# TensorE's order of an edge-gated graph layer, spread over one more block of edges

## The chip, the cores and the metric

One core of a Trainium2 chip runs the whole program. The metric is the device time of one execution in microseconds, the median of the runs. The engines are named as in the profile: PE (TensorE, matmuls), PEld (its weight loads), DVE (VectorE), ACT (ScalarE), POOL (GpSimd), SP (SyncE, which issues DMAs).

## The reference

A graph of 12,500 nodes (64 features) and 412,500 edges (32 features), sorted by destination. Cut to what matters:

```python
h  = relu(layernorm(x))
h0 = edge_attr @ W0 + b0
t  = gelu(gelu(h0) @ W1 + b1) @ W2 + b2
score = (h0 + t) @ W3 + b3                 # one row of 64 per edge
msg   = h[src] * score
sums  = segment_sum(msg, dst); cnt = segment_sum(1, dst)
out   = x + (sums / max(cnt, 1)) @ Wo + bo
```

## The kernel before

The edges are cut into NB = 403 blocks of 1,024 (8 tiles of 128). W2 and W3 are folded into one matrix `w_last` at the start. The layer norm of all nodes is made first and stored to `h_dram`; then the blocks are worked through one after the other. For block b:

- `first(b)` (PE, line 438): W0 times the block's attributes, into one of two PSUM banks `ps_h0a`, `ps_h0b` by parity. It raises `h0_done`. ACT's first gelu (line 392) turns it into `g1`.
- `second(b)` (PE, line 444): W1 times `g1`, into `ps_h1a`, `ps_h1b`. It raises `h1_done`. ACT's second gelu (line 397, two halves) writes rows 0 to 63 of `act_in`; the attributes themselves lie below them.
- `last(b)` (PE, line 453): 8 pairs of weight load and matmul that make the scores in `ps_sa`, `ps_sb`. It raises `score_done`. DVE multiplies them with the gathered rows of h (`message`, line 638) and raises `msg_done`.
- `summed(b)`, here `narrow` (PE, lines 465 and 472): waits for `msg_done` of b and for `added` of b - 1, then sums the messages of the block over a window of 64 destinations with a one-hot matrix (DVE, line 630), two tiles per matmul, into the one PSUM bank `ps_w`, and counts with two more matmuls. It raises `sums_done`. DVE's `add_window` (lines 739 to 750) adds the bank to the accumulator `acc` in SBUF and raises `added`.
- POOL gathers the 1,024 rows of h of a block with 8 indirect DMAs (line 334), into a ring of 16 blocks. The 8 gathers of block b + 16 wait for `msg_done` of b and for `score_done` of b + 8: so POOL may be at most 8 blocks ahead of the scores.
- SP loads the attributes twice, as `pair` (for `first`) and as rows of `act_in` (for `last`), each into a ring of 4.

The order on each engine is written out by hand and all waits are on semaphores. PE runs its steps in a loop of four blocks per turn. In a step b, PE does `second(b)`, `first(b + 1)`, `summed(b - 1)`, `last(b)`. DVE does one-hot of b, `add_window(b - 1)`, `message(b)`. ACT does the first gelu of b, then the second of b. After block 391 (EARLY_BLOCKS) PE projects the finished nodes (`project_early`), and then the last 12 blocks are worked through; the last gathers lie just after that projection.

## Time and profile before

| | |
|---|---|
| median of 3 runs | 4828.14 us (4825.08 to 4829.34) |
| the profiled execution: its own time | 4832.18 us |
| its span, first to last instruction | 4830.4 us |
| PE busy | 4044.0 us, 84% |
| POOL busy | 3051.3 us, 63% |
| DVE busy | 1046.3 us, 22% |
| ACT busy | 860.3 us, 18% |
| mean granted TensorE clock | 0.586 of full speed |

The profile tells when an instruction began, and for how long it ran; behind an instruction stands for how long the engine had been idle before it, and what ended that idle time. Where the profile finds nothing that raised the semaphore just then, it writes "remote". On one core there is no other core: "remote" then means that the semaphore was seen later than the end that the profile gives to the instruction that raises it.

### The profile page before, as it was taken

Reading aid. Unit: us, or ns where it says so; the run is one execution under the profiler, and the core shown is the slowest. Engines: PE = TensorE matmul, PEld = TensorE weight load, DVE = VectorE, ACT = ScalarE, POOL = GpSimd, SP = SyncE. Lnnn points to the kernel's source line nnn. Section 1 sums busy time; section 2 is a strip of 40 time slices with the busy share of each in tenths; the row PEclk is TensorE's granted clock in tenths of the full one; section 3 lists DMA queues with packets and bytes.
Section 4 is the critical chain, followed back from the end, with each engine's and each line's share of the span. In section 5 each row is a group of like instructions: output and inputs, shape, how many; then the busy total and the mean of one; then the engine's idle time right before and its main releaser. Section 6 shows DMA issues by size and latency. Waiting matters only on the chain.

```text
span 4830.4 us, 36572 instructions
## 1 busy us (share of the span) xinstructions
PE 4044.0 (84%) x12302; PEld 2563.7 (53%) x12303; DVE 1046.3 (22%) x2559; ACT 860.3 (18%) x1233; POOL 3051.3 (63%) x3228
## 2 busy tenths in 40 slices
PE   3888888888888888888888888888888888888889
PEld 1555555555555555555555555555555555555565
DVE  5212122212122212122212122212122212122232
ACT  3111111111111111111111111111111111111101
POOL 6666666666666666666666666666666666666641
PEclk9999997555555555555555555555555555555555
DMA  5222122212211211112221122212112212111211
GB/s 126 47 45 45 45 45 46 47 45 45 45 46 45 47 45 45 45 45 46 46 46 45 45 45 46 47 45 45 45 45 46 47 45 45 45 46 45 47 29 48
DMA packets 223807, 227.54 MB, mean 47 GB/s; under 512 B 118540, under 2 KB 118669, under 8 KB 223352
## 3 DMA queue, kind: packets, MB, share of 16 engines
q0 software_dynamic: 103136, 105.82, 11.7%
q1 hardware_dynamic: 119968, 117.76, 8.7%
q10 hardware_dynamic: 616, 3.20, 0.2%
q14 instruction: 80, 0.66, 0.0%
q8 instruction: 7, 0.11, 0.0%
HBM read 220.11 MB, written 6.40 MB: 47 GB/s over the span
## 4 chain that ended last, share of the span: by engine, by line
another core or an unknown queue 42%; PE 40%; issue 10%; DVE 8%; DMA 0%; ACT 0%; DVEq 0%; SPq 0%
PE ps_sb L453 14%; PE ps_w L465 12%; PE ps_w L472 5%; PE ps_h0b L438 4%; DVE msg L638 4%; PE ps_h1a L444 3%; DVE ln_sq L630 2%; DVE acc L745 1%; PE ps_sa L453 0%; PE ps_h1b L507 0%; PE ps_h1a L507 0%; DVE cnt_new L739 0%; DVE acc L750 0%; DVE ln_d L605 0%
## 5 line engine op out<-in xcount | busy, mean ns | idle before, releaser
L334 POOL DMA_INDIRECT rows<-h_rows,idx x3175 | 3005.4, 947 | 1682.9 <-issue 907.6
L465 PE MATMUL ps_w<-ln_sq,msg 128*128 128x128 f32 x3224 | 834.9, 441 | 692.4 <-DVE msg L638 686.5
L465 PEld LDWEIGHTS ps_w<-ln_sq,msg 128*128 128x128 f32 x3224 | 717.5, 327 | 1303.5 <-issue 1284.5
L453 PEld LDWEIGHTS ps_sb<-w_last,act_in 97*128 97x128 f32 x3216 | 701.1, 330 | 87.3 <-issue 87.3
L453 PEld LDWEIGHTS ps_sa<-w_last,act_in 97*128 97x128 f32 x3232 | 693.2, 325 | 89.2 <-issue 89.2
L453 PE MATMUL ps_sb<-w_last,act_in 97*128 97x64 f32 x3216 | 738.9, 424 | 0.0
L453 PE MATMUL ps_sa<-w_last,act_in 97*128 97x64 f32 x3232 | 730.8, 419 | 1.7 <-issue 1.7
L397 ACT ACTIVATE act_in<-ps_h1b,wp 64x512 f32<-64x512 f32 x402 | 274.8, 684 | 2351.0 <-remote 2307.9
L739 DVE TENSOR_REDUCE cnt_new<-ps_w 1x64 f32<-1x256 f32 x403 | 170.1, 422 | 1730.0 <-PE ps_w L472 974.5
L397 ACT ACTIVATE act_in<-ps_h1a,wp 64x512 f32<-64x512 f32 x404 | 276.3, 684 | 1424.9 <-issue 896.0
L638 DVE TENSOR_TENSOR msg<-ps_sa,rows 128x512 f32<-128x512 f32 x202 | 139.7, 692 | 1475.2 <-remote 1462.3
L444 PE MATMUL ps_h1b<-g,wp 128*128 128x512 f32 x402 | 400.6, 1099 | 32.6 <-issue 32.6
L444 PE MATMUL ps_h1a<-g,wp 128*128 128x512 f32 x404 | 408.4, 1114 | 14.0 <-issue 12.3
L438 PE MATMUL ps_h0b<-pair,wp 64*128 64x512 f32 x402 | 416.5, 1138 | 0.0
L438 PE MATMUL ps_h0a<-pair,wp 64*128 64x512 f32 x404 | 412.8, 1123 | 0.0
L630 DVE TENSOR_TENSOR ln_sq<-dst_i,ps_c 128x512 f32<-128x512 f32 x403 | 272.9, 677 | 1.0 <-issue 1.0
L438 PEld LDWEIGHTS ps_h0b<-pair,wp 64*128 64x128 f32 x402 | 100.3, 310 | 302.4 <-issue 302.4
L438 PEld LDWEIGHTS ps_h0a<-pair,wp 64*128 64x128 f32 x404 | 99.6, 306 | 298.1 <-issue 297.9
L638 DVE TENSOR_TENSOR msg<-ps_sb,rows 128x512 f32<-128x512 f32 x201 | 139.1, 692 | 489.8 <-PE ps_sb L453 438.9
L472 PE MATMUL ps_w<-ln_sq,ones_b 128*1 128x256 bf16 x806 | 235.2, 393 | 0.0
L745 DVE TENSOR_TENSOR acc<-acc,ps_w 64x64 f32 x806 | 176.3, 219 | 25.1
L392 ACT ACTIVATE g<-ps_h0b,wp 128x512 f32<-128x512 f32 x201 | 138.3, 688 | 120.0 <-PE ps_h0b L438 70.4
(65 smaller groups left out, 753.0 us busy)
## 6 DMA issues: line engine op xcount, KB each, us to landing
pair<-in_edges SPq DMA_DIRECT2D x403, 128.0 KB
act_in<-in_edges SPq DMA_DIRECT2D x403, 128.0 KB
rows<-h_rows,idx POOLq DMA_INDIRECT x3175
xs<-in_x SPq DMA_DIRECT2D x4, 700.0 KB
h_rows<-ln_d ACTq DMA_DIRECT2D x4, 700.0 KB
dst_i<-in_dst SPq DMA_DIRECT2D x1, 1612.0 KB
idx<-in_src SPq DMA_DIRECT2D x50, 32.0 KB
rows<-in_dst_rows SPq DMA_DIRECT2D x4, 384.0 KB
```

What stands on the lines that cost most here:

```text
L334: pool.indirect_dma_start(rows[:, slot, t, :], None, table, bass.IndirectOffsetOnAxis(ap=idx[:, part, at, t:t + 1], axis=0),).then_inc(gat ...
L392: act.activation(g1[:, s % 2, :], ps_h0[s % 2][:, :], ACT.Gelu, bias=b0).then_inc(g1_done, 1)
L397: act.activation(act_in[0:D, s % IN_RING, g, :], ps_h1[s % 2][g * D:(g + 1) * D, :], ACT.Gelu, bias=wp[g * D:(g + 1) * D, C_B1:C_B1 + 1]). ...
L438: pe.matmul(ps_h0[s % 2][:, :], w0, pair[:, s % IN_RING, :], start=True, stop=True).then_inc(h0_done, 1)
L444: pe.matmul(ps_h1[s % 2][:, :], w1, g1[:, s % 2, :], start=True, stop=True).then_inc(h1_done, 1)
L453: mm = pe.matmul(ps_s[s % 2][:, t * D:(t + 1) * D], act_in[:, s % IN_RING, g, j * P:(j + 1) * P], w_last[:, :], start=(t == 0), stop=(t == ...
L465: pe.matmul(window[0:m * D, 0:m * WIN], msg[:, s % 2, t:t + m, :].rearrange("p t d -> p (t d)"), hot[:, k, t:t + m, :].rearrange("p t n -> ...
L472: last = pe.matmul(window[D:DC, CNT:CNT + m], ones_b[:, :], hot_b[:, k, 2 * at + 1:2 * (at + m):2], start=(q == 0), stop=(q == 1), skip_gr ...
L630: return dve.tensor_tensor(to, rel.unsqueeze(2).to_broadcast([P, TILES, WIN]), iota_tiles, ALU.is_equal)
L638: dve.tensor_tensor(msg[:, s % 2, 0:n, :], ps_s[s % 2][:, 0:n * D].rearrange("p (t d) -> p t d", d=D), rows[:, s % G_RING, 0:n, :], ALU.mu ...
L739: return dve.tensor_reduce(cnt_new[D:DC, k, :], counts.rearrange("o (t n) -> o n t", n=WIN), AX_X, ALU.add)
L745: return dve.tensor_tensor(place, place, ps_w[h * D:(h + 1) * D, h * WIN:(h + 1) * WIN], ALU.add)
```

## The change

In a step b, PE now does `second(b)`, `first(b + 2)`, `summed(b - 3)`, `last(b - 1)`. The first layer runs two blocks ahead of the second, not one; the scores come one step after the second layer, and the sums three steps behind. ACT's gelus are split in two functions and ordered second(b), first(b + 2). DVE does `add_window(b - 2)`, one-hot of b, `message(b)`. SP asks for the `pair` of b + 6 where it asked for that of b + 4. The rings, the two buffers of each PSUM tile, the one bank `ps_w`, POOL's order and its waits, and every instruction's shape stay as they are. The core of the diff:

```diff
             def ahead(b, s):
-                sp.wait_ge(h0_done, b + 1)
-                load_pair(b + IN_RING, s + IN_RING)
+                if b + IN_RING + 2 < NB:
+                    sp.wait_ge(h0_done, b + 3)
+                    load_pair(b + IN_RING + 2, s + IN_RING + 2)
...
+            gelu_first(1, 1)
+            gelu_second(1, 1)
+            gelu_first(2, 2)
+            gelu_first(3, 3)
+            for b in range(2, NB):
+                gelu_second(b, b)
+                if b + 2 < NB:
+                    gelu_first(b + 2, b + 2)
...
                 def step(b, s):
                     second(b, s)
-                    first(b + 1, s + 1)
-                    summed(b - 1, s - 1)
-                    last(b, s)
+                    first(b + 2, s + 2)
+                    summed(b - 3, s - 3)
+                    last(b - 1, s - 1)
...
             last(0, 0)
             second(1, 1)
             first(2, 2)
+            first(3, 3)
+            second(2, 2)
+            first(4, 4)
             last(1, 1)
+            second(3, 3)
+            first(5, 5)
...
                 narrow(0, 0)
-                steps(2, EARLY_BLOCKS + 1, narrow)
+                last(2, 2)
+                steps(4, EARLY_BLOCKS + 3, narrow)
+                pe.wait_ge(g2_done, (EARLY_BLOCKS + 3) * 2)
                 project_early()
...
                 def step(b, s):
+                    if s > 1:
+                        add_window(b - 2, s - 2)
                     one_hot(hot[:, s % 2, :, :], rel_of(b))
-                    add_window(b - 1, s - 1)
                     message(b, s)
```

On PE, one step of the loop before, with the semaphores that each waits for (`ps_w` is the sum of a block, `ps_sb` a score):

```order
L444 MATMUL ps_h1b<-g,wp 128x512 [waits g1_done]
L437 ISA
L438 MATMUL ps_h0a<-pair,wp 128x512 [waits pair_in0]
L486 REGISTER_ALU [waits msg_done]
L465 MATMUL ps_w<-ln_sq,msg 128x128 [waits added]
L465 MATMUL ps_w<-ln_sq,msg 128x128 x3
L472 MATMUL ps_w<-ln_sq,ones_b 1x256 x2
L450 REGISTER_ALU [waits attr_in3]
L453 MATMUL ps_sb<-w_last,act_in 128x64 [waits g2_done]
L453 MATMUL ps_sb<-w_last,act_in 128x64 x7
```

and a step of the loop now:

```order
L457 MATMUL ps_h1b<-g,wp 128x512 [waits g1_done]
L450 ISA
L451 MATMUL ps_h0b<-pair,wp 128x512 [waits pair_in3]
L499 REGISTER_ALU [waits msg_done]
L478 MATMUL ps_w<-ln_sq,msg 128x128 [waits added]
L478 MATMUL ps_w<-ln_sq,msg 128x128 x3
L485 MATMUL ps_w<-ln_sq,ones_b 1x256 x2
L461 ISA
L463 REGISTER_ALU [waits attr_in0]
L466 MATMUL ps_sa<-w_last,act_in 128x64 [waits g2_done]
L466 MATMUL ps_sa<-w_last,act_in 128x64 x7
```

The kinds follow one another as before; what moved is the block that each belongs to. The first layer now has the parity of the second (`ps_h0b` beside `ps_h1b`), since it is two blocks ahead and no longer one, and the score has the other parity (`ps_sa`), since it is a block behind.

On DVE, one block before (`cnt_new` and `acc` are `add_window`, `ln_sq` is the one-hot matrix):

```order
L630 TENSOR_TENSOR ln_sq<-dst_i,ps_c 128x512
L755 TENSOR_LOAD base_b
L739 TENSOR_REDUCE cnt_new<-ps_w 1x64 [waits sums_done]
L745 ISA [waits added]
L745 TENSOR_TENSOR acc<-acc,ps_w 64x64
L750 ISA [waits cnt_summed]
L750 TENSOR_TENSOR acc<-acc,cnt_new 1x64
L745 TENSOR_TENSOR acc<-acc,ps_w 64x64 [waits added]
L638 TENSOR_TENSOR msg<-ps_sa,rows 128x512 [waits gathered10,score_done]
```

and now:

```order
L780 TENSOR_LOAD base_b
L764 TENSOR_REDUCE cnt_new<-ps_w 1x64 [waits sums_done]
L770 ISA [waits added]
L770 TENSOR_TENSOR acc<-acc,ps_w 64x64
L775 ISA [waits cnt_summed]
L775 TENSOR_TENSOR acc<-acc,cnt_new 1x64
L770 TENSOR_TENSOR acc<-acc,ps_w 64x64 [waits added]
L655 TENSOR_TENSOR ln_sq<-dst_i,ps_c 128x512
L663 TENSOR_TENSOR msg<-ps_sa,rows 128x512 [waits gathered10,score_done]
```

The one-hot matrix now comes behind `add_window`, which belongs to the block two before, and just ahead of the message.

## Rows read from the trace of the kernel before

**Rows 1.** the page: busy time of each engine, and the costliest group of POOL
```profile
PE 4044.0 (84%) x12302; PEld 2563.7 (53%) x12303; DVE 1046.3 (22%) x2559; ACT 860.3 (18%) x1233; POOL 3051.3 (63%) x3228
...
L334 POOL DMA_INDIRECT rows<-h_rows,idx x3175 | 3005.4, 947 | 1682.9 <-issue 907.6
```

**Rows 2.** the waits: engine and line, what ended them, us in total, times, longest
```profile
DVE msg L638 <- remote: 1469.3, 198, 16.4
...
POOL rows L334 <- DVE msg L638: 757.8, 194, 51.7
```

**Rows 3.** timeline, 3013 to 3038: start, us, what, count [idle before <-releaser]
```profile
3013.20 0.69 DVE L638 TENSOR_TENSOR msg<-ps_sa,rows 128x512 f32<-128x512 f32 x1 [7.30 <-remote]
...
3014.03 2.07 PE L465 MATMUL ps_w<-ln_sq,msg 128*128 128x128 f32 x8 [3.44 <-DVE msg L638]
...
3016.54 3.68 PE L453 MATMUL ps_sb<-w_last,act_in 97*128 97x64 f32 x16
...
3020.01 2.02 PE L444 MATMUL ps_h1a<-g,wp 128*128 128x512 f32 x2
...
3020.26 0.69 DVE L638 TENSOR_TENSOR msg<-ps_sb,rows 128x512 f32<-128x512 f32 x1 [2.44 <-PE ps_sb L453]
...
3021.96 2.07 PE L438 MATMUL ps_h0b<-pair,wp 64*128 64x512 f32 x2
...
3023.97 2.07 PE L465 MATMUL ps_w<-ln_sq,msg 128*128 128x128 f32 x8
...
3026.48 3.68 PE L453 MATMUL ps_sa<-w_last,act_in 97*128 97x64 f32 x16
...
3028.07 0.42 DVE L739 TENSOR_REDUCE cnt_new<-ps_w 1x64 f32<-1x256 f32 x1 [6.52 <-PE ps_w L472]
...
3029.01 0.22 DVE L745 TENSOR_TENSOR acc<-acc,ps_w 64x64 f32 x1
...
3029.95 2.02 PE L444 MATMUL ps_h1b<-g,wp 128*128 128x512 f32 x2
...
3031.90 2.07 PE L438 MATMUL ps_h0a<-pair,wp 64*128 64x512 f32 x2
...
3036.59 0.69 DVE L638 TENSOR_TENSOR msg<-ps_sa,rows 128x512 f32<-128x512 f32 x1 [7.35 <-remote]
...
3037.41 2.07 PE L465 MATMUL ps_w<-ln_sq,msg 128*128 128x128 f32 x8 [3.44 <-DVE msg L638]
```

**Rows 4.** timeline of POOL there: first and last of 16 gathers, the next
```profile
3013.92 0.94 POOL L334 DMA_INDIRECT rows<-h_rows,idx  x1 [3.69 <-DVE msg L638]
...
3032.67 0.95 POOL L334 DMA_INDIRECT rows<-h_rows,idx  x1 [0.31 <-issue]
3037.30 0.95 POOL L334 DMA_INDIRECT rows<-h_rows,idx  x1 [3.69 <-DVE msg L638]
```

**Rows 5.** timeline, 104 to 117: a burst of 8 gathers, the answer after
```profile
104.88 0.94 POOL L334 DMA_INDIRECT rows<-h_rows,idx  x1 [8.90 <-remote]
...
113.64 0.94 POOL L334 DMA_INDIRECT rows<-h_rows,idx  x1 [0.30 <-issue]
...
116.44 0.69 DVE L638 TENSOR_TENSOR msg<-ps_sa,rows 128x512 f32<-128x512 f32 x1 [5.87 <-remote]
...
116.68 0.95 POOL L334 DMA_INDIRECT rows<-h_rows,idx  x1 [2.10 <-remote]
```

**Rows 6.** windows, no gathers: us, PE, PEld, DVE, ACT, POOL, PEclk
```profile
4757.00:4811.00 54.00, 54.00 (x171) 35.04 (x170) 12.89 (x34) 10.28 (x15) 0.00 (x0) 0.50 0.24 69
```

**Rows 7.** timeline of DVE in that stretch: two messages, one block apart
```profile
4761.53 0.69 DVE L638 TENSOR_TENSOR msg<-ps_sa,rows 128x512 f32<-128x512 f32 x1 [2.43 <-PE ps_sa L453]
...
4771.48 0.69 DVE L638 TENSOR_TENSOR msg<-ps_sb,rows 128x512 f32<-128x512 f32 x1 [2.44 <-PE ps_sb L453]
```

**Rows 8.** timeline 1998 to 2009: one scoring group at half the usual time
```profile
1998.05 2.00 PE L453 MATMUL ps_sa<-w_last,act_in 97*128 97x64 f32 x16
...
2008.16 0.69 DVE L638 TENSOR_TENSOR msg<-ps_sa,rows 128x512 f32<-128x512 f32 x1 [8.03 <-remote]
```

More of the change, by code:

```diff
@@ L303, in group_ahead @@
                 load_idx(group + IDX_GROUPS, part, n)
+            for b in range(2):
+                sp.wait_ge(h0_done, b + 1)
+                load_pair(b + IN_RING, b + IN_RING)
             for group in range(GROUPS - IDX_GROUPS):
@@ L387, in clear_acc, with gelu_first @@
                                ).then_inc(acc_zero, 1)
-            def gelus(b, s):
+            def gelu_first(b, s):
                 act.wait_ge(h0_done, b + 1)
@@ L393, in gelus, with gelu_second @@
                                ).then_inc(g1_done, 1)
+            def gelu_second(b, s):
                 act.wait_ge(h1_done, b + 1)
@@ L417, in _ @@
             act.wait_ge(weights_in, 16)
-            gelus(0, 0)
+            gelu_first(0, 0)
+            gelu_second(0, 0)
             for k in range(LN_STEPS, len(jobs) + 1):
@@ L423, in _ @@
                     ln_root(k - 1, *jobs[k - 1])
-            for b in range(1, NB):
-                gelus(b, b)
+            gelu_first(1, 1)
[6 more added lines that the diff above has]
+                    gelu_first(b + 2, b + 2)
         @block.tensor
@@ L526, in step @@
                     second(b, s)
-                    first(b + 1, s + 1)
-                    summed(b - 1, s - 1)
-                    last(b, s)
+                    first(b + 2, s + 2)
+                    summed(b - 3, s - 3)
+                    last(b - 1, s - 1)
                 blocks_loop(pe, first_block, end, IN_RING, step)
             def finish(summed):
-                second(NB - 1, NB - 1)
+                for b in (NB - 2, NB - 1):
+                    second(b, b)
+                    summed(b - 3, b - 3)
+                    last(b - 1, b - 1)
+                summed(NB - 3, NB - 3)
+                last(NB - 1, NB - 1)
                 summed(NB - 2, NB - 2)
-                last(NB - 1, NB - 1)
                 summed(NB - 1, NB - 1)
@@ L553, in _ @@
                 narrow(0, 0)
-                steps(2, EARLY_BLOCKS + 1, narrow)
+                last(2, 2)
+                steps(4, EARLY_BLOCKS + 3, narrow)
+                pe.wait_ge(g2_done, (EARLY_BLOCKS + 3) * 2)
                 project_early()
-                steps(EARLY_BLOCKS + 1, NB - 1, narrow)
+                steps(EARLY_BLOCKS + 3, NB - 2, narrow)
                 finish(narrow)
@@ L559, in _ @@
                 wide(0, 0)
-                steps(2, NB - 1, wide)
+                last(2, 2)
+                steps(4, NB - 2, wide)
                 finish(wide)
@@ L776, in program_narrow @@
                 bias_late()
-                for b in range(2, EARLY_BLOCKS + 1 - BIAS_STEPS):
+                for b in range(2, EARLY_BLOCKS + 2 - BIAS_STEPS):
                     step(b, b)
                 for k in range(BIAS_STEPS):
-                    b = EARLY_BLOCKS + 1 - BIAS_STEPS + k
+                    b = EARLY_BLOCKS + 2 - BIAS_STEPS + k
                     step(b, b)
@@ L785, in program_narrow @@
                 output_early()
-                for b in range(EARLY_BLOCKS + 1, NB):
+                for b in range(EARLY_BLOCKS + 2, NB):
                     step(b, b)
+                add_window(NB - 2, NB - 2)
                 add_window(NB - 1, NB - 1)
```

## The prediction

> **What bounds the kernel now.** I began with the busy shares: PE 84%, POOL 63% in gathers of 947 ns, DVE and ACT about a fifth each [rows 1]. PE looks like the bound, with a little to win. The waits then say something else: the longest named waits of DVE's messages are on "remote", 1469.3 us in 198 times, and POOL waits 757.8 us in 194 times, 3.9 us each, for what lies just before the message [rows 2]. Both occur in every second block, so I read two blocks of the timeline [rows 3].
>
> The reader is to see a cycle of two blocks there: a message at 3013.20 and the same kind again at 3036.59, 23.39 us, or 11.70 us a block. From start to start, PE's four groups take 1.95 (second, 3020.01 to 3021.96), 2.01 (first), 2.51 (sums with counts) and 3.47 us (last), together 9.94 us a block; twice that is 19.9, and the rest is the 3.44 us that PE is idle before 3037.41 [rows 3]. But the idle time isn't a queue of dependent work of that length. The scores `ps_sb` end at 3020.22 by their row, and the message starts at 3020.26. The scores `ps_sa` end at 3030.16 by theirs, and the message starts at 3036.59, 6.4 us late. The second layer between them, over at 3031.97, was done earlier than that too. So in the second half of each cycle what PE has finished is not seen by the others. Even `sums`, over at 3026.55, is answered 1.5 us late, at 3028.07 [rows 3].
>
> What ends the lateness? POOL. Its 16 gathers run from 3013.92 to 3033.62, one each 1.25 us (18.75 us from the first start to the last), and the late answers come 2.97 us after the last one [rows 4, 3]. Near the start, a burst of only 8 gathers ends at 114.58, and the answer comes at 116.44, 1.86 us after it [rows 5]. And where no gather runs at all, messages are 9.95 us apart, PE is busy 54.00 of 54 us, and nothing is late [rows 6, 7]. One more row excludes that PE's own work sets the time: at 1998.05 a scoring group takes 2.00 us instead of 3.68, and yet the message comes at 2008.16, 8 us after its end [rows 8], at the same place in the cycle.
>
> So the loop is this: released scores let POOL do 8 gathers each; while POOL gathers without a pause, PE's answers come late after some 12 us; the burst ends only when POOL runs out of released scores; then all late answers come at once. For a burst of n blocks the cycle is 0.71 us (message 3036.59 to the next gather 3037.30) + 10.0 n - 0.3 + the delay after the burst. With 1.86 for n = 1 and 2.97 for n = 2 the delay is 0.75 + 1.11 n. The cycle is then 1.16 + 11.11 n: 12.27, 23.38 (measured: 23.39), 34.49, 45.6 us, that is 12.27, 11.69, 11.50, 11.40 us a block. The last two are estimates beyond the rows.
>
> **The change, part by part.** No instruction is added or removed; each block still has the same matmuls, gelus, loads and gathers. What changes is how much PE work lies between an operation and the one that needs its answer. Score to sums: before second + first, 3.96 us; now second, first, sums, last, second, first, 13.9 us. Second layer to last: before 4.5, now first, sums, last, second, first, sums, 14.5 us. First to second: before 6.0, now 15.9 us. A message takes 0.69 us, so each of these can be some 13 us late and cost nothing. One distance stays: sums of a block must be added by DVE (3028.07 to 3029.23, 1.16 us) before the next sums overwrite the only bank, and between them lie last, second, first, 7.4 us, before and now. That leaves 6.2 us for lateness. The sums' answer is 1.5 us late in the cycle shown, so it fits; a sums' answer held to the end of the burst doesn't.
>
> So follow PE from a release at 0, in the new order. Where it stands before sums whose predecessor waits to be added, it resumes at 1.2 us. Then a block of 9.94 to 11.1 (answered on time: today's answers are prompt up to the `first` that ends 10.8 us after the release), a second block to 21.1 (its sums end at 13.7 and are answered 1.5 us late, at 15.2, added by 16.4), a third block to 31.0, whose sums at 21.1 could start for just that reason. The fourth sums need the third's answer, which is held. So PE gets through three blocks in one cycle, not two. Three scores (at 7.2, 17.1, 27.1) are released in each cycle; POOL does 24 gathers; the cycle is 34.49 us, and PE with 31.0 us fits into it. 3.44 us of idle time a cycle stays, but it comes once in three blocks. Saved: 11.695 - 11.497 = 0.198 us a block. Of the 403 blocks, 388 are in this stretch (block 2 is at 116.44 [rows 5]; the projection comes after block 391): 388 x 0.198 = 77 us.
>
> The rest is small. At the start three groups more stand before the second score, 2.0 + 1.95 + 2.0 = 6.0 us; but POOL was idle 8.9 us there, until 104.88 [rows 5], for late answers rather than for work: between 0 and +6, I take +3. The new wait before the projection is for gelus of a `second` issued three groups (8.0 us) earlier; PE has waited for the accumulator there anyway: 0, or 1.4 us if that cover is gone. On SP, the `pair` load of a block still waits for the `first` four blocks before it, and the attribute load for the score four blocks before it, so both leads stay some 40 us, and the order of the two on SP is the same: 0. On ACT and DVE the new order puts nothing behind a wait that its reader needs sooner: DVE's message of b stands behind `add_window(b - 2)`, whose sums PE makes before the scores of b. The last 12 blocks have no gathers to speak of and no idle PE: 0. Sum: 4832.2 (the profiled execution) - 77 + 3 = 4758; that execution is 4.0 us above the median of the runs, so **4754 us**.
>
> The rule that speaks for much more is in the Trainium skill, TensorE: Matmul & The Clock Gate, "Why this matters for your kernels": without idle gaps TensorE keeps the full clock. The row is against it: PE busy 54.00 of 54 us, and the granted clock 0.50 [rows 6], which is 1.2 GHz. By the rule PE's work would halve and POOL's 10.0 us a block be the bound, which is the second rival's time; by the row PE stays at 9.94 us.
>
> **Rivals.** (1) The cycle of 16 gathers stays: if the second block's sums are answered only with the rest, PE stops at 21.1 us, two scores are released each cycle, and POOL's 23.4 us remain. It decides at a lateness of 6.2 us. For it: the lateness of sums could grow when PE comes in another phase; against it: 1.5 us in the row. Time 4828, within 5. (2) The lateness doesn't matter any more, as all but one distance are 14 us: POOL's pace of 10.0 us a block, 388 x 1.69 = 656 us less, 4175 us. For it: 9.95 us a block without gathers [rows 7]. Against it: the lateness ended only after the burst, and with POOL at 10.0 and PE at 9.94 no burst would end. Between both lie bursts of four and more blocks: 11.40 gives 4718, the limit 11.11 gives 4605. (3) Slower: PE no longer stands still at the end of a burst, so its scores no longer fall at 7 us after the release but anywhere. If one comes later than 10.4 us (0.71 + 9.7), POOL ends after 8 gathers, at 12.27 us a block instead of 11.69. With one such cycle beside each one of 16, the mean is (12.27 + 23.39) / 3 = 11.89: +75 us, 4903; with all of them +223, 5051. It decides as soon as one cycle of 8 comes for each three or so of 24 (cost 0.58 us against 3 x 0.198). For it: both lengths occur before [rows 4, 5]; against it: with three scores a cycle two are always held over to the release.
>
> **How the numbers follow.** Cycles mostly of 24 gathers, alone or mixed with 16 (4735 to 4818): 0.46. The old cycle (within 0.2%, 4818 to 4838; about what a measurement can tell from no change): 0.20. Longer bursts, 4605 to 4735: 0.06. POOL's pace: 0.06. Slower: 0.22, of which half beyond 4880. So faster 0.58, same 0.20, slower 0.22. The range is 4650 to 4880, which leaves out POOL's pace, the longest bursts, and the upper half of rival 3, under 2 in 10.
>
> **What would show it.** Right: 24 gathers between two long pauses of POOL, the pauses some 34.5 us apart; PE idle once in three blocks; scores answered late in two blocks of three; PE's groups still 1.95 to 3.47 us. The old cycle would show 16 gathers and PE stopped at `ps_w` for an adding of DVE; rival 2, POOL busy without pauses; rival 3, bursts of 8. The forecast is wrong above all if the lateness isn't bound to the bursts: then my delay of 0.75 + 1.11 n, from two points, means nothing.

## The result

The changed kernel takes **4798.37 us** (median of 10 runs, 4792.93 to 4804.45), the kernel before in the same hour 4827.95 us (10 runs). The ratio is 0.9946, 95% interval 0.9934 to 0.9958: 0.54% or 30 us faster, where 74 us were forecast. The direction is right, the size is not.

The page of the changed kernel, with the rows that answer to [rows 1] (columns as there):

```profile
PE 3983.9 (83%) x12302; PEld 2530.1 (53%) x12303; DVE 1073.6 (22%) x2559; ACT 858.8 (18%) x1233; POOL 3048.6 (64%) x3228
...
L478 PE MATMUL ps_w<-ln_sq,msg 128*128 128x128 f32 x3224 | 823.8, 436 | 694.2 <-DVE acc L770 680.6
```

Its waits (us in total, times, longest), which answer to [rows 2]:

```profile
DVE cnt_new L764 <- remote: 1251.1, 80, 21.0
DVE msg L663 <- remote: 1218.0, 161, 15.8
...
PE ps_w L478 <- DVE acc L770: 680.6, 62, 18.8
```

PE is idle for about as long as before, but in 62 pieces, not 197, and no longer for a message: it waits for the adding of the one window bank. And a new late answer stands above the message: `cnt_new`, DVE's first work on finished sums. ("Remote" says only that the trace has no semaphore event just then. That an answer is late is read from the starts of the instructions that wait.)

Between two pauses POOL now makes 16 gathers in 116 cycles, 24 in 51, and 8 in 6 (counted over POOL's rows from 120 us on, a pause from 0.6 us; before, 16 in 194 and 8 in one). The rows at the pauses, and what PE, DVE and ACT do between them, on the timeline of the changed kernel:

```profile
3012.32 0.95 POOL L338 DMA_INDIRECT rows<-h_rows,idx  x1 [3.70 <-DVE msg L663]
...
3015.38 0.69 DVE L663 TENSOR_TENSOR msg<-ps_sa,rows 128x512 f32<-128x512 f32 x1 [1.17 <-PE ps_sa L466]
...
3021.61 3.68 PE L466 MATMUL ps_sb<-w_last,act_in 97*128 97x64 f32 x16
...
3034.91 0.69 DVE L663 TENSOR_TENSOR msg<-ps_sb,rows 128x512 f32<-128x512 f32 x1 [11.30 <-remote]
...
3035.62 0.94 POOL L338 DMA_INDIRECT rows<-h_rows,idx  x1 [3.62 <-DVE msg L663]
...
3041.49 2.00 PE L466 MATMUL ps_sb<-w_last,act_in 97*128 97x64 f32 x16
...
3046.47 0.39 PE L485 MATMUL ps_w<-ln_sq,ones_b 128*1 128x256 bf16 x2
...
3047.65 0.69 DVE L663 TENSOR_TENSOR msg<-ps_sb,rows 128x512 f32<-128x512 f32 x1 [4.16 <-remote]
...
3050.45 0.18 PEld L451 LDWEIGHTS ps_h0a<-pair,wp 64*128 64x128 f32 x1 [0.64 <-issue]
3050.47 1.39 ACT L403 ACTIVATE act_in<-ps_h1b,wp 64x512 f32<-64x512 f32 x2 [10.70 <-issue]
...
3053.28 0.69 ACT L396 ACTIVATE g<-ps_h0b,wp 128x512 f32<-128x512 f32 x1 [1.42 <-remote]
...
3068.67 0.42 DVE L764 TENSOR_REDUCE cnt_new<-ps_w 1x64 f32<-1x256 f32 x1 [20.33 <-remote]
...
3069.89 2.07 PE L478 MATMUL ps_w<-ln_sq,msg 128*128 128x128 f32 x8 [18.15 <-DVE acc L770]
3070.22 0.94 POOL L338 DMA_INDIRECT rows<-h_rows,idx  x1 [4.93 <-issue]
```

The reader is to see one cycle of 16 gathers (3012.32 to 3035.62) and one of 24 (3035.62 to 3070.22). In the first, the scores `ps_sb` end 13.0 us after the first gather and their message comes only after the burst. In the second they end 7.9 us after it and their message comes at 3047.65, still during the burst: that is the third release, and POOL goes on. The price stands in the same cycle: the sums that end at 3046.86 are answered at 3068.67, 21.8 us late, and PE stands still for 18.15 us. Such a stop (12.3 us in the mean) stands in all 51 cycles of 24, and in 10 of the 116 of 16. One thing is not usual in the cycle shown: from 3041.49 PE works at the higher level of its clock (a scoring group in 2.00 us). Of the 51 scores that prolong a burst only 4 were made at it.

**Where the 30 us are.** From the 201st to the 3001st gather the cycles take 11.629 us a block instead of 11.685, and the last gather begins at 4729.1 instead of 4750.6. So the cycles give some 21 us. Behind the last gather the profiled execution is 12.8 us shorter (67.0 against 79.8 us), with as many matmuls. A row of each kernel's windows shows a higher granted clock in that stretch (third number from the end; first the changed kernel, then the kernel before, then the changed kernel once more, run `a_same` below):

```profile
4729.00:4796.00 67.00, 57.18 (x230) 38.84 (x228) 20.93 (x55) 10.94 (x16) 0.94 (x1) 0.60 0.21 60
```
```profile
4751.00:4830.00 79.00, 68.81 (x226) 44.86 (x224) 20.35 (x55) 13.70 (x20) 0.56 (x1) 0.52 0.19 54
```
```profile
4756.00:4796.00 40.00, 30.23 (x197) 22.81 (x196) 18.63 (x49) 8.90 (x13) 0.77 (x1) 0.88 0.33 93
```

The changed order also runs the blocks of this stretch, so it is not outside the change. In the three traces of the new order on occasions of this kind the stretch takes 67.0, 40.4 and 65.9 us (granted clock 0.60, 0.88, 0.60; the second has 30 matmuls less to do), in the three of the old order with the same matmuls in a block 79.8, 79.8 and 79.3 us (0.52, 0.54, 0.50). Whether the order brings the higher clock there, or chance, was not tried.

### The profile page after: what moved, and what is told of

The parts are those of the page before. It is cut to its first block, busy times and chain, and to the rows that moved or that the text cites. A ratio compares the mean times of both kernels' runs of the same rounds, so it can differ in the third digit from the quotient of the medians.

```text
span 4796.1 us, 36452 instructions
## 1 busy us (share of the span) xinstructions
PE 3983.9 (83%) x12302; PEld 2530.1 (53%) x12303; DVE 1073.6 (22%) x2559; ACT 858.8 (18%) x1233; POOL 3048.6 (64%) x3228
## 4 chain that ended last, share of the span: by engine, by line
PE 46%; another core or an unknown queue 39%; issue 8%; DVE 5%; DVEq 1%; DMA 0%; SPq 0%
PE ps_w L478 11%; PE ps_sa L466 8%; PE ps_sb L466 8%; PE ps_h0a L451 4%; PE ps_h0b L451 4%; PE ps_h1a L457 4%; PE ps_h1b L457 4%; PE ps_w L485 3%; DVE ln_sq L655 2%; DVE msg L663 1%; DVE acc L770 1%; DVEq L780 1%; DVE cnt_new L764 1%; PE ps_h1a L520 0%
## 5 line engine op out<-in xcount | busy, mean ns | idle before, releaser
L478 PE MATMUL ps_w<-ln_sq,msg 128*128 128x128 f32 x3224 | 823.8, 436 | 694.2 <-DVE acc L770 680.6
L478 PEld LDWEIGHTS ps_w<-ln_sq,msg 128*128 128x128 f32 x3224 | 707.0, 323 | 1287.5 <-DVE acc L770 758.9
L466 PEld LDWEIGHTS ps_sb<-w_last,act_in 97*128 97x128 f32 x3216 | 685.6, 323 | 98.9 <-issue 97.0
L466 PE MATMUL ps_sb<-w_last,act_in 97*128 97x64 f32 x3216 | 724.7, 416 | 11.8 <-issue 11.6
L396 ACT ACTIVATE g<-ps_h0a,wp 128x512 f32<-128x512 f32 x202 | 138.8, 687 | 117.4 <-issue 46.3
```

What stands on the lines that cost most here:

```text
L396: act.activation(g1[:, s % 2, :], ps_h0[s % 2][:, :], ACT.Gelu, bias=b0).then_inc(g1_done, 1)
L466: mm = pe.matmul(ps_s[s % 2][:, t * D:(t + 1) * D], act_in[:, s % IN_RING, g, j * P:(j + 1) * P], w_last[:, :], start=(t == 0), stop=(t == ...
L478: pe.matmul(window[0:m * D, 0:m * WIN], msg[:, s % 2, t:t + m, :].rearrange("p t d -> p (t d)"), hot[:, k, t:t + m, :].rearrange("p t n -> ...
```

## The experiments

The kernel before was timed anew beside each group of runs, and that brought a surprise: it took 4828, 4861 and 4831 us on three occasions, but 4093, 4097, 4089 and 4089 us on four others, with the same program. The record names a chip for all but the first: 6 and 2 for the late ones, 6, 7, 13 and 13 for the others. So it isn't the chip alone: chip 6 gave 4093 us and, 14 minutes later, 4861 us. I call the first kind a late occasion (PE's answers are late) and the second a prompt one. Several kernels were run again because they had met only prompt occasions.

### What the change is worth where nothing is late

The changed kernel itself, on a prompt occasion:

> The changed kernel, unchanged. So far it has been timed only on occasions where the kernel before takes 4828 and 4861 us (ratios 0.9946 and 0.9924). Two other occasions had the kernel before at 4093 and 4097 us, gathers without a pause. Theory A (all of the gain is room for late answers): there the same within 0.2%, POOL at 10.0 us a block; on an occasion of the late kind 0.992 to 0.995 again, with bursts of 16, 24 and some of 8. Rival B (the order saves something by itself): 0.992 to 0.995 on either.

Measured: 4077.22 us (12 runs) against 4089.33 us, ratio 0.9995 [0.997, 1.002]. The medians lie 12 us apart, but the kernel before varies from 4050 to 4092 us here, and the interval holds no difference. Rows of its page, and the first of its waits:

```profile
PE 3961.2 (97%) x12302; PEld 2516.3 (62%) x12303; DVE 1084.0 (27%) x2559; ACT 860.2 (21%) x1233; POOL 3045.7 (75%) x3228
...
POOL rows L338 64%; PE ps_w L478 3%; PE ps_sb L466 3%; PE ps_sa L466 2%; PE ps_h0a L451 1%; PE ps_h0b L451 1%; PE ps_h1a L457 1%; PE ps_h1b L457 1%; PE ps_w L485 1%; PE ps_h1a L520 1%; PE ps_h1b L520 1%; POOLq L359 0%; DMA rows<-in_x,idx 0%; DMA rows<-h_rows,idx 0%; DMA idx<-in_src 0%
```
```profile
DVE msg L663 <- DMA rows<-h_rows,idx: 2468.1, 336, 8.0
```

Here the messages wait for gathered rows, not for "remote"; the chain that ended last is 64% gathers, which follow each other without a pause at 9.99 us a block. That is the state of rival 2, reached without the change. No gain is seen where nothing is late, as theory A says, and rival B's 0.992 to 0.995 is out.

Three edits were meant to take PE's load up and down, and one part of the change back, and fell on prompt occasions. Their edits, in this order: 16 tiny matmuls behind the counts; every other score tile only; sums two steps behind instead of three.

```diff
+TINY = 16
...
+                for q in range(TINY):
+                    last = pe.matmul(window[D:DC, CNT + 256:CNT + 257], ones_b[:, :],
+                                     hot_b[:, k, 1:2], start=True, stop=True,
+                                     skip_group_check=True)
```
```diff
-                for t in range(TILES):
+                for t in range(0, TILES, 1 if s < 2 else 2):
```
```diff
-                    summed(b - 3, s - 3)
+                    summed(b - 2, s - 2)
```

> Kernel before, with 16 matmuls of one column (and their weight loads) behind the counts of each block, 32 more PE instructions to the 60 of a block and an estimated 1 us. Theory A with a lateness that begins a time after the burst's start (12 us): PE's 3.44 us of idle time per two blocks cover it, 4828 within 10. Theory A with a lateness that begins after a number of PE instructions (60 to 80): the second score of a cycle comes late as well, bursts fall to 8 gathers at 12.27 us a block, up to 5051. Theory B: the time of the added instructions on top, near 5200.

> Kernel before, but from block 2 on `last` makes 4 of the 8 score tiles; the other four keep old values. PE has 1.73 us less work in a block (half of 3.47), 8.2 us instead of 9.94. Theory A (a block costs what the cycle of POOL's bursts costs, 1.16 + 11.11 n us for n blocks, whatever PE does): 4828 within 10 us if bursts stay at 16 gathers; if fewer PE instructions in a block let more answers through in a burst, some bursts of 24 and down to 4750. Theory B (PE's work and its waits add up to the block): 388 x 1.73 = 671 us less, 4157.

> Changed kernel with one part undone: PE sums block b - 2 in step b, not b - 3, so that between a score and its sums lie second and first (3.96 us) as before; the first layer two ahead, the score one step late, ACT's, DVE's and SP's order as in the changed kernel. Theory A: the late score stops PE as before, bursts of 16 only, PE idle 3.4 us in two blocks, 4828 within 8. Rival (the gain is that of the first layer two ahead, or of DVE's order): 4798 within 8.

The second round of the three, when the starving rows of the two-bank kernel (below) were known:

> The kernel before with 16 one-column matmuls more behind the counts of each block (some 0.4 us of PE's time, 32 more PE instructions with their weight loads beside the 61 of a block). Nothing is left out. It ran once where no answer was late (4093 us before, 1.003 of it). In the rows where PE starves with two banks, PE starts one instruction each 0.70 us until the gathers end. Where answers are late (the kernel before takes 4828 to 4861 us): theory A (PE's instructions are answered at a pace of so many instructions, not of so much time) says that with 93 instead of 61 a block the score comes later than 10.4 us behind the release in many cycles, bursts of 8 gathers at 12.3 us a block, 4920 to 5090 us; rival B (the answers are held by time, whatever their number) says cycles of 16 gathers as before, within 0.2% of the kernel before. Where the kernel before takes 4093 us both say 1.003 again.

> The kernel before with only 4 of the 8 score tiles from block 2 on (the other tiles keep old values): 16 PE instructions and 1.6 to 1.8 us less a block, 45 instead of 61. Where answers are late: theory A (so many instructions) says that the third block's score of a cycle is answered before the gathers end or PE's backlog is gone sooner, bursts of 24 or more, 4560 to 4780 us; rival B (by time) says that the cycle is set by gathers and the delay behind them, 16 gathers and 23.4 us, within 0.3% of the kernel before. Where the kernel before takes 4093 us: 4074 us, ratio 0.997, as in its first run.

> The changed kernel with the sums two steps behind the second layer instead of three: score to sums is 3.96 us of PE's work again, as in the kernel before; the second layer and the score keep their new distances. Nothing is left out. Its first run fell where no answer was late (ratio 1.0007). Where answers are late: theory A (one short distance is enough to stop PE; with the sums alone moved it was 0.997) says cycles of 16 gathers throughout and 0.997 to 1.000 of the kernel before; rival B (the distances of the second layer and the score bring the gain, the sums' does not) says bursts of 24 among those of 16 and 0.991 to 0.995.

And the third:

> The kernel before with 16 one-column matmuls more behind the counts of each block: some 0.4 us of PE's time and 32 more PE instructions beside 61. Nothing is left out. Where answers are late (the kernel before at 4828 to 4861 us): theory A (PE's instructions are answered at a pace of so many instructions) says the scores are later than 10.4 us behind the release in many cycles, bursts of 8 gathers, 4920 to 5090 us; rival B (held by time, whatever their number) says cycles of 16 as before, within 0.2%. Where the kernel before takes some 4095 us: 1.002 to 1.003 as on two such occasions.

> The kernel before with only 4 of the 8 score tiles from block 2 on (the other tiles keep old values): 45 PE instructions a block instead of 61, 1.6 to 1.8 us less. Where answers are late (the kernel before at 4828 to 4861 us): theory A (PE is answered at a pace of so many instructions) says bursts of 24 or more among those of 16, 4560 to 4780 us; rival B (held by time alone) says 16 gathers and 23.4 us a cycle, within 0.3% of the kernel before. Where the kernel before takes some 4095 us: 0.995 to 0.997, as twice before.

> The changed kernel with the sums two steps behind the second layer instead of three (score to sums 3.96 us of PE's work again). Nothing is left out. Where answers are late: theory A (one short distance is enough to stop PE) says cycles of 16 gathers throughout, 0.997 to 1.000 of the kernel before; rival B (the distances of the second layer and the score bring the gain) says bursts of 24 among those of 16 and 0.991 to 0.995. Where the kernel before takes some 4095 us: 1.001, as twice before.

| | median | against before there | ratio |
|---|---|---|---|
| tiny matmuls, three occasions | 4100.37, 4099.98, 4096.56 | 4093.22, 4096.90, 4089.33 | 1.0031 [1.0003, 1.0058], 1.0022, 1.0041 |
| half of the scores, three | 4073.77, 4077.87, 4070.11 | 4093.22, 4096.90, 4089.18 | 0.9967 [0.9937, 0.9996], 0.9952, 0.9961 |
| near sums, three | 4091.48, 4097.20, 4088.86 | 4093.22, 4096.90, 4089.18 | 1.0007 [0.9978, 1.0035], 1.0009, 1.0023 |

They say only that at POOL's pace PE's load and order weigh next to nothing. The expectations of the first round were all made for late answers and missed by some 700 us; where those of the later rounds gave a number for this kind of occasion, it held within 0.2%. The half scores and the near sums never met a late occasion, so what they would do there is open.

### Is it the gathers that hold the answers?

```diff
-                for t in range(tiles_of(b)):
+                for t in range(TILES) if b < G_RING else range(0, TILES, 2):
                     pool.indirect_dma_start(
...
-                dve.wait_ge(gathered[s % G_RING], (uses(b, G_RING) - 1) * 16 * TILES + 16 * n)
+                dve.wait_ge(gathered[s % G_RING], (uses(b, G_RING) + 1) * 16 * TILES // 2)
```

> The kernel before with only 4 of the 8 gathers of each block from block 16 on (half of the source rows stay what they were); the changed kernel with the same cut took 2522 and 2494 us (5.30 us a block with PE at double speed and never idle), where the kernel before, whole, takes 4093 to 4097 us. Theory A (the order matters only for late answers; at double speed second and first take 2.0 us, still more than the message's 0.7): 2450 to 2600 us, like the changed order. Rival B (the short distances stop PE now and then, its clock falls, and PE at 9.94 us a block binds): 3000 to 3950 us, and the change would be worth hundreds of us in such a kernel. On an occasion where answers are late (the kernel before at 4828 to 4861 us): if only unbroken gathers hold the answers, none is late here and the time is as in A; if not, over 3900 us.

This one met a late occasion: 3900.22 us (3868.66 to 3990.79, 5 runs) where the kernel before took 4831.53. Its waits, and a block of its timeline (its profiled execution is the longest of the five):

```profile
DVE cnt_new L739 <- PE ps_w L472: 1652.6, 336, 6.1
...
DVE msg L638 <- PE ps_sb L453: 451.2, 190, 2.6
```
```profile
2001.22 3.68 PE L453 MATMUL ps_sb<-w_last,act_in 97*128 97x64 f32 x16
...
2004.93 0.69 DVE L638 TENSOR_TENSOR msg<-ps_sb,rows 128x512 f32<-128x512 f32 x1 [2.44 <-PE ps_sb L453]
...
2014.87 0.69 DVE L638 TENSOR_TENSOR msg<-ps_sa,rows 128x512 f32<-128x512 f32 x1 [2.22 <-PE ps_sa L453]
```

The scores end at 2004.90 and the message starts at 2004.93. With 4 gathers and then a pause in each block next to nothing is late, in the old order, on an occasion of the late kind, and the cycle is PE's 9.94 us. That is theory A's mechanism with rival B's time: I had expected 2450 to 2600 us with nothing late, but PE, never stopped for long, works at 1.2 GHz.

The trace holds its own comparison. Up to 186 us, while POOL still makes bursts of 16, the answers are late as in the kernel before. Behind that they are late in seven short places only. In each of these the granted clock is 1.00 for 34 to 41 us (457.2 to 491.3 us in the first), a block takes 5.3 us, and POOL's 5.0 us of gathers come 8 in a row. Then the answers are late, PE stops, and the clock is at 0.50 again:

```profile
457.00:476.00 19.00, 19.00 (x110) 12.38 (x108) 7.10 (x18) 6.16 (x9) 11.22 (x12) 0.99 0.26 62
```
```profile
472.92 0.39 PE L472 MATMUL ps_w<-ln_sq,ones_b 128*1 128x256 bf16 x2
...
476.35 0.42 DVE L739 TENSOR_REDUCE cnt_new<-ps_w 1x64 f32<-1x256 f32 x1 [5.08 <-remote]
...
478.73 1.15 PE L465 MATMUL ps_w<-ln_sq,msg 128*128 128x128 f32 x8 [1.52 <-DVE msg L638]
```

The sums that end at 473.31 are answered 3.0 us late, 10 us behind the first of the 8 gathers (466.42). So it takes both, the occasion and gathers that follow one another for longer than the 4.7 us of a burst of 4. Whether it is their pause that counts, or their number in a time, isn't told apart by this cut. The same cut in the changed kernel had run on a prompt occasion:

> Changed kernel, but from block 16 on POOL makes 4 of a block's 8 gathers; the other rows are those of an earlier block. POOL needs 5.0 us in a block instead of 10.0. Theory A (gathers without a pause make PE's answers late): bursts of 4, no late answers, PE's 9.94 us a block: 4798 - 388 x (11.63 - 9.94) = 4142. Rival (PE's answers are late because PE itself works without a pause): nothing changes in PE's work, 4750 to 4830.

Repeated, in the hope of a late occasion, which did not come:

> The changed kernel with only 4 of the 8 gathers of each block from block 16 on (half of the source rows stay what they were), so that POOL gathers 5 us a block and pauses in between. Where no answer was late it took 2356 to 2549 us at a granted clock of 0.98, 5.3 to 5.8 us a block. Theory A (the answers are late because gathers follow each other without a pause): where the kernel before takes 4828 to 4861 us nothing is late here, and the time is 2350 to 2560 us as on the other occasion. Rival B (a property of the occasion holds PE's answers, whatever POOL does): lateness stays, PE is slower than 9.94 us a block or near it, 3900 us or more. Middle case: bursts stay short but PE's clock stays at 1.2 GHz for want of the first warm stretch, 3850 to 3950 us with nothing late.

2522.22 us (2356.06 to 2548.79) the first time, and 2493.97 us (2396.94 to 2558.26) the second, four executions each; in the profiled one of 2356.06 us a block takes 5.30 us. A window of it and one scoring group:

```profile
300.00:2200.00 1900.00, 1900.00 (x10753) 1229.88 (x10752) 879.16 (x2149) 737.38 (x1077) 1354.55 (x1435) 1.00 0.32 75
```
```profile
1505.71 2.00 PE L466 MATMUL ps_sb<-w_last,act_in 97*128 97x64 f32 x16
```

PE is busy all of 1900 us at the higher level, 2.4 GHz. Here pauses of only 0.6 us lie between POOL's gathers of one block and the next, and no wait of the whole trace ended on "remote". So the same cut gave both levels of the clock, with two orders on two kinds of occasion. The seven places above speak for the occasion: the old order reached the same 5.3 us a block there, and late answers ended it each time. No run had both orders on one kind of occasion, so this isn't shown.

### By number of instructions, or by time?

The tiny matmuls at last met a late occasion; their 16 matmuls with their weight loads raise PE's instructions from 61 to 93 a block and its time by 0.4 us.

> The kernel before with 16 one-column matmuls more behind the counts of each block, 32 PE instructions more beside 61. Nothing is left out. Where answers are late (the kernel before at 4828 to 4861 us): theory A (PE is answered at a pace of so many instructions) says bursts of 8 in many cycles, 4920 to 5090 us; rival B (held by time) says cycles of 16 as before, within 0.2%. Where the kernel before takes some 4095 us: 1.002 to 1.004, as three times before.

4918.12 us (4898.07 to 4925.05) against 4831.53, ratio 1.0173 [1.0145, 1.0202]. That is 2 us below theory A's range and 77 us above rival B's. Where the old kernel has 16 gathers between pauses, this one has 8 in every one of its 391 cycles, 12.07 us each in the median and 11.92 us a block in the mean; the pauses are shorter, 0.9 to 1 us in 89 of them and mostly 1.5 to 3.5 us in the others. Theory A: 0.4 us of work can't do that. The timeline of its PE, matmuls and then weight loads, in a burst:

```profile
3029.15 0.48 PE L454 MATMUL ps_sb<-w_last,act_in 97*128 97x64 f32 x2 [0.93 <-issue]
...
3029.86 0.27 PE L454 MATMUL ps_sb<-w_last,act_in 97*128 97x64 f32 x1 [0.22 <-issue]
...
3031.25 0.27 PE L454 MATMUL ps_sb<-w_last,act_in 97*128 97x64 f32 x1 [1.13 <-issue]
```
```profile
3030.55 0.29 PEld L454 LDWEIGHTS ps_sb<-w_last,act_in 97*128 97x128 f32 x1 [0.90 <-issue]
3031.27 0.29 PEld L445 LDWEIGHTS ps_h1a<-g,wp 128*128 128x128 f32 x1 [0.43 <-issue]
```

PE waits for no semaphore here ("issue"), and yet starts one instruction each 0.70 us. The same pace is in the changed kernel's answers above: from the message at 3047.65 (scores answered) to the gelu at 3050.47 (the four instructions of `second`) 2.82 us, and to the gelu at 3053.28 (the four of `first`) 2.81 us, 0.70 us for each instruction. The 20 of sums and counts then need 15.4 us, to 3068.67, which is 0.77 us each. So while gathers run without a pause, PE's instructions are answered one each 0.70 to 0.77 us, after a first stretch in which all is prompt. That stretch has no fixed length. In the kernel before, the sums that end 12.6 us after the first gather are the first late ones; in the cycle above, the score that ends 7.9 us after it is 4.2 us late already.

### Which stop holds the cycles down?

Two edits tell: the window sums in two banks in turn (the iota and the bias then lie elsewhere), tried in both orders, and the sums moved alone, in the old order.

```diff
-                sums(b, s, ps_w, s % 2).then_inc(sums_done, 1)
+                sums(b, s, ps_w[s % 2], s % 2).then_inc(sums_done, 1)
...
-                    pe.wait_ge(added, b * 3)
+                    pe.wait_ge(added, (b - 1) * 3)
...
-        iota = ps_c[:, 0:WIN]
+        iota = sb("iota_f", [P, WIN])[:, :]
```
```diff
                     second(b, s)
                     first(b + 1, s + 1)
-                    summed(b - 1, s - 1)
+                    summed(b - 2, s - 2)
                     last(b, s)
```

In the second edit DVE's `add_window` also comes a block later and ahead of the one-hot, as in the change. They ran together with the changed kernel on one late occasion:

> The changed kernel, unchanged, timed again, because the kernel before takes 4828 us on one chip and 4093 us on another. Theory A (the gain is made of late answers: PE's order has more room for answers that are held while GpSimd gathers): where the kernel before takes 4828 us, this takes 4795 to 4802 us and its gathers come in bursts of 16, 16, 24; where it takes 4093 us, GpSimd's gathers already follow each other without a pause, no answer is late, and this takes the same within 0.2% (4085 to 4101 us). Rival B (the new order saves something by itself, at the start or in PE's waits for gelus): 0.5 to 0.7% faster on either chip, 4065 to 4073 us where the kernel before takes 4093.

> The changed kernel with the window sums in two banks in turn, so that PE's sums of a block wait for DVE's adding of the block two before, not of the last one (17 us of PE's work between them, not 7.4). Nothing is left out; the iota and the bias are read from elsewhere. Theory A (PE's stop at the one window bank is what holds the cycles to 16 and 24 gathers), where the kernel before takes 4828 us: no stop of PE at ps_w of over 1 us, all bursts of 24 gathers or more, 11.4 to 11.5 us a block, 4720 to 4760 us. Rival B (the bursts are set by when POOL finds a released score, not by PE's stop): bursts of 16 and 24 as now, 4790 to 4805 us. Where the kernel before takes 4093 us both say the same within 0.3%, since the gathers bind at 10.0 us a block.

> The kernel before with the window sums in two banks in turn; nothing is left out. Its distances between score, message and sums stay at 3.96 us. Theory A (one late score is enough to stop PE in the old order, the bank doesn't matter there), where the kernel before takes 4828 us: cycles of 16 gathers and 23.4 us as before, 4820 to 4836 us. Rival B (the wait for the bank is what stops PE in the old order too): 4750 to 4800 us. Where the kernel before takes 4093 us: the same within 0.3% by both.

> One part of the change alone: the kernel before with the sums two steps behind the second layer instead of one (score to sums 13.9 us of PE's work, not 3.96), second layer and first layer left where they were, so that the score of a block still follows 4.5 us behind its second layer. Nothing is left out. Theory A (all three distances must be long, as any late answer stops PE), where the kernel before takes 4828 us: the score waits for a gelu whose layer was answered late, cycles of 16 gathers stay, 4815 to 4835 us. Rival B (only the distance from score to sums matters, because score and message are the late ones in the row): 4790 to 4805 us, like the whole change. Where the kernel before takes 4093 us: the same within 0.3% by both.

| against before at 4861.25 | median | ratio | cycles of 8, 16, 24 | mean gather |
|---|---|---|---|---|
| the change | 4827.70 | 0.9924 [0.9911, 0.9938] | 23, 139, 30 | 947 ns |
| the change, two banks | 4818.22 | 0.9901 [0.9886, 0.9916] | 4, 45, 99 | 967 ns |
| before, two banks | 4912.34 | 1.0104 [1.0089, 1.0120] | 1, 193, 1 | 974 ns |
| before, sums moved | 4846.80 | 0.9971 [0.9959, 0.9983] | 1, 195, 0 | 947 ns |

The cycles are those of one profiled execution each; for the change it is the fastest of its five, 4798.01 us. The sums alone keep the cycle of 16, and 0.3% is what they give; a row of its waits names the next stop, the score that waits for its gelu:

```profile
PE ps_sa L453 <- ACT act_in L397: 701.2, 195, 8.2
```

So moving the sums isn't enough while another distance is short, as theory A says. The second bank does nothing for the old order's cycles, and its gathers are dearer, 974 instead of 947 ns; the kernel takes 51 us more. The edit brings DVE's one-hot from an operand in PSUM to two in SBUF, and that is where the gathers lose:

```profile
3017.43 0.68 DVE L630 TENSOR_TENSOR ln_sq<-dst_i,iota_f 128x512 f32<-128x512 f32 x1
3017.53 1.39 POOL L334 DMA_INDIRECT rows<-h_rows,idx  x1 [3.71 <-DVE msg L638]
3019.23 0.94 POOL L334 DMA_INDIRECT rows<-h_rows,idx  x1 [0.30 <-issue]
```

The gathers that overlap a one-hot take 1175 ns in the mean there, the others 944; in the kernel before both kinds take 946. By the Trainium skill, SBUF — State Buffer, "SBUF: two separate sides", a DVE instruction with two SBUF inputs and a GpSimd instruction that reads SBUF exclude each other at a shared port. The rows agree with it, as the gathers read their indices `idx` from SBUF. No run moved the iota alone. So its time missed both expectations, while its cycles are theory A's. In the new order the bank turns most cycles into ones of 24 (not all, as theory A had it), and against the old order with the same banks that is 4818 to 4912, 1.9%. Its own time met neither expectation: 0.9901 of the kernel before would be 4780 us on the first occasion, between theory A's 4720 to 4760 and rival B's 4790 to 4805. But in place of PE's stop at `ps_w` comes another. Two of its PE weight loads, a DVE row between them:

```profile
3034.47 0.28 PEld L466 LDWEIGHTS ps_sb<-w_last,act_in 97*128 97x128 f32 x1 [2.02 <-issue]
...
3035.88 0.28 PEld L466 LDWEIGHTS ps_sb<-w_last,act_in 97*128 97x128 f32 x1 [1.11 <-issue]
3035.89 0.42 DVE L763 TENSOR_REDUCE cnt_new<-ps_wa 1x64 f32<-1x256 f32 x1 [18.31 <-remote]
```

At 3035.88 PE starts the third instruction of a scoring group, and at 3035.89 the sums of the block before last are answered. Between the two lie 32 instructions of a score, 4 and 4 of `second` and `first`, 20 of sums and counts, and 2 or 3: 62 or 63. In the changed kernel it is the same number: at 3050.45 PE starts the third instruction of a `first`, and at 3050.47 the `second` before the last is answered, with 4 + 20 + 32 + 4 + 2 or 3 between them. PE gets that far ahead of its answers, and no farther. The Trainium skill, TensorE: Matmul & The Clock Gate, "Architectural detail: the array is 16× 32×32, not 1× 128×128", gives the depth of TensorE's queue as 64; the count agrees with it, as an explanation that no run tested by itself.

## Why the prediction was wrong in its size

**What held.** The bound: POOL's released gathers and PE's late answers, and not PE's own work. The mechanism of the gain: more room between a score, its message and the sums, so that a third score is released within a cycle. The lengths: 23.36 us for 16 gathers (23.38 by the formula), 34.71 for 24 (34.49), 12.07 for 8 with the tiny matmuls (12.27 was taken). The start: the gathers are level with those of before at 289 us (289.3 and 289.5), where +3 us were taken. The measured 4798 also lies in the first band of the forecast, cycles of 24 "mixed with 16 (4735 to 4818)"; 4754 is the number for 24 throughout. The row at 1998.05 was read rightly too: in the kernel before, the six cycles in which a scoring group ran at double speed took 23.33 to 23.41 us, the others 23.37 in the median.

**The step that failed** is "So PE gets through three blocks in one cycle, not two", and with it the 77 us. It was worked out for one cycle from a fixed phase, with the sums "answered 1.5 us late" wherever they fall. The term was worth 21.5 us (the last gather at 4729.1 instead of 4750.6 us), for two reasons:

- The cycle of 24 costs 34.71 us: 388 x (11.685 - 11.57) = 45 us, even if every cycle were one.
- Only 51 of 173 are. Over POOL's and PE's rows, the score that decides (the next one behind those already released) ends 15.1 us after a cycle's first gather in the cycles of 16, in the median (12.2 to 16.5 for eight in ten), and 9.6 us in those of 24 (8.9 to 10.3). A score that ends within some 12 us is answered during the burst, though some us late (4.5 in the median), and prolongs it; a later one is held to its end. In a cycle of 16 PE, never stopped now, gains 23.4 - 19.9 = 3.5 us on POOL, so its scores fall near 16.5, 13, 9.6, and the third cycle gets 24. In that one the sums are answered at 0.70 to 0.77 us an instruction, PE stands at `ps_w` (18.15 us in the row, 12.3 in the mean) and loses the lead. Hence 16, 16, 24, the usual sequence: seven blocks in 2 x 23.36 + 34.71 = 81.4 us, 11.63 a block.

A second term was mis-sized: "The last 12 blocks have no gathers to speak of and no idle PE: 0". The stretch behind the last gather took 12.8 us less, at a granted clock of 0.60 instead of 0.52. Without it the profiled executions would lie 21 us apart, not 34; the part of it that is luck is open.

The first of these two is rival 1's mechanism, "the second block's sums are answered only with the rest, PE stops", in one cycle of three instead of in all; the forecast took the two as alternatives, and they take turns. The argument for "1.5 us in the row" was the false one: lateness isn't a length of time but a backlog of instructions that grows by PE's phase. That the phase decides was read from rows, and the two-bank kernel bears it out: without the stop at `ps_w`, 99 cycles of 24 and 45 of 16.

**Rival 2** was weighed by the wrong test. Its pace of 10.0 us a block is reached on prompt occasions, with either order, and at 1.2 GHz; no row of the kernel before could show that. **Rival 3**, bursts of 8, came in 6 cycles here, in 23 on another occasion, and in all 391 with the tiny matmuls. Its break-even was worked out wrongly: the gain of 3 x 0.198 us is that of one cycle of 24, so one cycle of 8 (0.58 us) eats one of 24, not three.

**What stays open:** what makes an occasion late. The one other difference seen is in the record: on prompt occasions the page of a kernel with all gathers pairs them with their landings (2.4 us in the median), on late ones it pairs none. The trace tells why: each gather raises its semaphore 16 times, and of the 51,568 events of POOL's 3,223 gathers a prompt trace holds 51,567, the late ones of the kernel before and after 10,358 and 9,903. Whether the paths of these events are what holds PE's answers was not tried. A rival stands untested here: each execution on record has its clock and span from the profile, so no run tells whether recording the events takes part in the lateness. Nor did the half scores or the near sums meet a late occasion.

## What to carry to other kernels

A stretch of one cycle shows a phase, not a rule: before a gain is multiplied by the number of cycles, follow the model through three of them and see whether the phase comes back. Late answers ("remote" on one core) are a backlog: ask what it is counted in, and what it does to an engine that runs ahead. And time the kernel before on more than one occasion, since a change can be worth 0.5 to 0.8% on one and nothing on another.

## What the runs showed of the hardware

- With gathers without a pause, on some occasions, PE's instructions are answered one each 0.70 to 0.77 us, and PE stops some 62 or 63 instructions ahead. On other occasions the same kernel has nothing late and is 15% faster (4093 against 4828 us).
- 32 more PE instructions a block, 0.4 us of work, cost 1.7% there and 0.2 to 0.4% elsewhere.
- A gather that starts beside a one-hot with two operands in SBUF takes 1.39 us instead of 0.94.
- The granted clock doesn't always tell the speed. In the changed kernel's windows up to 1200 us it is 1.00, and a scoring group there takes as long as at 0.50 (15 matmuls 3.41 us, against 16 in 2.00 us at double speed). The mean granted clock of an execution holds such a stretch, so it tells little: 0.989 for the tiny matmuls' 4925 us, 0.586 for the kernel before.

```profile
500.00:510.00 10.00, 10.00 (x32) 6.34 (x31) 3.00 (x9) 3.57 (x6) 7.55 (x8) 1.00 0.27 76
```
```profile
499.76 3.41 PE L466 MATMUL ps_sa<-w_last,act_in 97*128 97x64 f32 x15
```
